# Rewritten units of a selective scan, with the gate behind the first scan of the next unit

## What is computed

```python
residual = hidden if residual is None else hidden + residual
hidden = rmsnorm(residual, norm_w[i])
# mamba_mixer: d = 64, dI = 128, 16 states, L = 256, batch 2
u, z = split(x @ in_w);  uc = silu(conv4(u) + cb)
dt_r, Bm, Cm = split(uc @ xp_w);  dt = softplus(dt_r @ dt_w + dt_b)
h = exp(dt * A) * h + (dt * u) * B_t;  y_t = einsum(h, C_t)     # over 256 steps
y = (y + u * Dp) * silu(z);  return y @ out_w
```

## Time and profile before

| | us |
|---|---|
| median of 3 runs | 383.29 |
| lowest, highest | 382.54, 387.21 |
| span of the profiled execution | 383.2 |
| VectorE busy | 291.4 (76%) |
| TensorE busy, weight loads | 321.3 (84%), 231.9 (61%) |
| ScalarE busy | 251.6 (66%) |
| GpSimd busy | 210.4 (55%) |

### The profile page before, as it was taken

How to read it: one execution, slowest core, us unless ns; L and a number is a source line. 1 busy time by engine, 2 the same in 40 slices (tenths; PEclk the granted TensorE clock), 3 DMA queues, 4 the chain that set the end, 5 groups by cost and what they waited for, 6 DMA issues and landing times.

```text
span 383.2 us, 5559 instructions
## 1 busy us (share of the span) xinstructions
PE 321.3 (84%) x1810; PEld 231.9 (61%) x1810; DVE 291.4 (76%) x508; ACT 251.6 (66%) x698; POOL 210.4 (55%) x182
## 2 busy tenths in 40 slices
PE   4866998899999998788979798797987979778674
PEld 3255775656557646566758576575856758556552
DVE  2675377868783525498988989899898998989453
...
GB/s 214 358 119 3 124 2 1 2 0 3 3 0 2 1 110 2 143 136 275 62 213 156 124 272 47 232 143 136 258 28 269 103 173 212 68 275 0 2 0 14
DMA packets 19750, 41.06 MB, mean 107 GB/s; under 512 B 7986, under 2 KB 10626, under 8 KB 19594
## 3 DMA queue, kind: packets, MB, share of 16 engines
...
HBM read 40.31 MB, written 0.39 MB: 106 GB/s over the span
## 4 chain that ended last, share of the span: by engine, by line
PE 37%; DVE 31%; POOL 11%; ACT 9%; issue 7%; DMA 2%; POOLq 1%; DVEq 0%; SPq 0%; ACTq 0%
DVE big L1148 14%; POOL big L1662 5%; PE PS L678 4%; PE PS L521 4%; DVE big L1139 4%; PE PS L291 2%; ACT PS L1460 2%; PE PS L297 2%; DVE big L1158 2%; PE PS L485 2%; POOL big L1563 2%; PE PS L415 2%; PE PS L585 2%; PE PS L495 2%; POOL rms L1638 2%
## 5 line engine op out<-in xcount | busy, mean ns | idle before, releaser
L1148 DVE TENSOR_TENSOR_SCAN big<-PS,big 128x1024 f32<-128x1024 f32 x48 | 108.4, 2281 | 1.0 <-DVE big L1139 0.2
L1460 ACT ACTIVATE PS<-unit_t,amat 128x255 f32<-128x255 f32 x192 | 81.6, 467 | 13.4 <-DVE unit_t L1123 9.0
L1671 POOL TENSOR_TENSOR big<-big 128x1024 f32<-128x1024 f32 x36 | 84.8, 2358 | 4.2 <-DVE big L1148 1.6
L678 PE MATMUL PS<-big,cst 128*128 128x256 f32 x288 | 66.5, 387 | 0.7 <-POOL big L1671 0.6
L678 PEld LDWEIGHTS PS<-big,cst 128*128 128x128 f32 x288 | 55.4, 194 | 9.9 <-POOL big L1671 2.2
L1662 POOL TENSOR_TENSOR big<-unit_t,big 128x1024 f32<-128x1024 f32 x24 | 57.4, 2396 | 5.7 <-issue 3.7
L1620 POOL TENSOR_TENSOR w2t<-w2t,w0t 128x768 f32<-128x768 f32 x2 | 3.6, 1807 | 92.3 <-DVE big L1078 92.3
L1264 ACT ACTIVATE big<-PS 128x512 f32<-128x512 f32 (+1 forms) x43 | 24.7, 583 | 25.2 <-PE PS L521 9.9
L646 PE MATMUL PS<-stack,pick_b 96*128 96x256 bf16 x144 | 22.2, 277 | 11.9 <-DVE big L1139 10.5
L1316 ACT ACTIVATE big<-PS,big 128x256 f32<-128x256 f32 x64 | 29.6, 473 | 1.5 <-DVE big L918 1.4
L1139 DVE TENSOR_TENSOR big<-unit_t,PS 128x1024 f32<-128x1024 f32 x24 | 29.0, 1208 | 0.5 <-PE PS L646 0.4
...
## 6 DMA issues: line engine op xcount, KB each, us to landing
...
```

Source lines behind the costliest of these rows:

```text
L678: pe.matmul(yps, ident, hc[:, g, s], start=False, stop=False)
L1148: v.tensor_tensor_scan(flat(hst[:, g]), flat(da[g % 2]), flat(dbu[:, g]), 0.0, ALU.mult, ALU.add).then_inc(sem("m_h"), 1)
L1460: one = act.activation(da[g % 2][:, n, 1:N], dt[u % 2][:, 1:N], ACT.Exp, scale=amat[:, u // 2, col:col + 1])
L1671: pool.tensor_tensor(hc[:, g], hst[:, g], csp[u % 2][:, SG * g:SG * (g + 1)], ALU.mult)\
```

## The change

VectorE: the gate of unit u - 1 moves from ahead of drive 0 to behind scan 0. softplus is approximated in another form: ScalarE does Abs, Tanh, Exp, Tanh instead of six operations, and VectorE one fused operation instead of two ahead of dt. dt now also waits until stack is complete.

TensorE: the transpose of hs is written as four plain f32 products (hs is no longer doubled to 128 columns; the second pair writes the shifted copy to partitions 64 to 127). The bf16 parts of xd are taken away in PSUM by `take_away`, between the sums. `spread_first` moves to the end of the unit before, `prep_in` behind `spread_last`, `sum_skip` ahead of the two idle products, and `sum_last` ahead of the second half of group 2's sum. `out_proj` of the unit before still stands ahead of `spread_second`.

ScalarE: hs is 64 columns wide, ht one operation for both halves of the partitions, each part of stack is one more copy of xd, and the decays stand in other places among them. GpSimd: `prep_split` goes, weigh 0 stands ahead of drive 3, and weigh 2 has two halves. The diff, without its constants, buffers, set-up on GpSimd and changed counts of semaphores:

```diff
@@ -618,7 +618,12 @@
-            last = pe.transpose(PS[:, 7, a * P:(a + 1) * P], hs2[b][:, a], ident)
+            one = hs2[b][:, a, 0:D]
+            pe.matmul(PS[0:D, 7, a * P:(a + 1) * P], one, ident, start=True, stop=True)
+            if a == 0:
+                last = pe.matmul(PS[D:P, 7, 0:P + 1], one, moved[:], start=True, stop=True)
+            else:
+                last = pe.matmul(PS[D:P, 7, P + 1:N], one, ident[:, 0:P - 1], start=True, stop=True)
@@ -637,6 +644,14 @@
+    def take_away(u, n):
+        pe.wait_ge(sem("m_xs"), 4 * u + 2 + n)
+        if n == 0:
+            pe.wait_ge(sem("m_sp"), 4 * u + 1)
+        pe.matmul(xd, less[:, n], stack[u % 2][:], start=False, stop=True, skip_group_check=True)\
+            .then_inc(sem("m_less"), 1)
@@ -663,27 +678,34 @@
-    def sum_skip(u, zs_of=None):
+    def sum_skip(u):
...
+        pe.wait_ge(sem("m_zs"), u + 1)
+        pe.matmul(yps, dmat[:, i], uc[b], start=True, stop=True)
+    def sum_y(u, g, zs_of=None):
+        pe.wait_ge(sem("m_hc"), 4 * u + g + 1)
...
-        pe.matmul(yps, dmat[:, i], uc[b], start=True, stop=False)
-    def sum_y(u, g):
-        pe.wait_ge(sem("m_hc"), 3 * u + g + 1)
...
-            pe.matmul(yps, ident, hc[:, g, s], start=False, stop=False)
+            pe.matmul(yps, ident, hc[:, g, s], start=False, stop=True, skip_group_check=True)
+    def sum_third(u, h):
+        pe.wait_ge(sem("m_hc"), 4 * u + 3 + h)
+        for s in range(2 * h, 2 * h + 2):
+            last = pe.matmul(yps, ident, hc[:, 2, s], start=False, stop=True, skip_group_check=True)
+        return last
     def sum_last(u):
...
-                last = pe.matmul(yps, ident, hc[:, NSG - 1, s], start=False, stop=(s == SG - 1))
-        last.then_inc(sem("m_y"), 1)
+                pe.matmul(yps, ident, hc[:, NSG - 1, s], start=False, stop=True, skip_group_check=True)
@@ -698,40 +720,56 @@
+    def idle_turns(count):
+        for _ in range(count):
+            pe.matmul(PS[:, 6, N:2 * N], zero_t[:, 0:1].to_broadcast([P, P]), CONST.of(cst, "rope")[:, 0:N],
+                      start=False, stop=True, skip_group_check=True)
     def keep_awake(count, bank=5):
...
     keep_awake(7, 6)
+    pe.wait_ge(sem("m_moved"), 4)
     prep_transpose(0)
     keep_awake(1)
     pe.wait_ge(sem("m_weights"), 5)
     prep_in(0)
     keep_awake(3)
     prep_x(0)
-    keep_awake(7)
+    take_away(0, 0)
+    keep_awake(1)
+    take_away(0, 1)
+    keep_awake(5)
+    spread_first(0)
     for u in range(UNITS):
         more = u + 1 < UNITS
         if u:
-            sum_y(u - 1, 2)
             sum_last(u - 1)
-        spread_first(u)
-        if u:
+            sum_third(u - 1, 1).then_inc(sem("m_y"), 1)
             out_proj(u - 1)
         spread_second(u)
+        sum_skip(u)
         if more:
-            keep_awake(2, 6)
+            idle_turns(2)
             prep_transpose(u + 1)
-            prep_in(u + 1)
         spread_last(u)
         if more:
+            prep_in(u + 1)
             prep_x(u + 1)
-        sum_skip(u, u + 1 if more else None)
-        sum_y(u, 0)
+        sum_y(u, 0, u + 1 if more else None)
+        if more:
+            take_away(u + 1, 0)
         sum_y(u, 1)
-    sum_y(UNITS - 1, 2)
+        if more:
+            take_away(u + 1, 1)
+        sum_third(u, 0)
+        if more:
+            spread_first(u + 1)
     sum_last(UNITS - 1)
+    sum_third(UNITS - 1, 1).then_inc(sem("m_y"), 1)
     out_proj(UNITS - 1)
     spare(1, 5)
@@ -1114,13 +1150,11 @@
     def prep_dt(u):
...
-        v.wait_ge(sem("m_sp"), 6 * u + 4)
-        v.scalar_tensor_tensor(sp_a, sp_3, LOG_D2, sp_u, ALU.add, ALU.mult).then_inc(sem("m_poly"), 1)
-        v.wait_ge(sem("m_sp"), 6 * u + 6)
-        v.wait_ge(sem("m_poly"), 2 * u + 1)
-        v.scalar_tensor_tensor(sp_v, sp_2, LOG_SCALE * LOG_D, sp_a, ALU.add, ALU.mult).then_inc(sem("m_poly"), 1)
-        v.wait_ge(sem("m_poly"), 2 * u + 2)
-        v.scalar_tensor_tensor(dt[b], dtp, 0.0, sp_v, ALU.max, ALU.add).then_inc(sem("m_dt"), 1)
+        v.wait_ge(sem("m_sp"), 4 * u + 4)
+        v.scalar_tensor_tensor(sp_l, sp_w, LOG_D / LOG_S, sp_u, ALU.add, ALU.mult).then_inc(sem("m_poly"), 1)
+        v.wait_ge(sem("m_poly"), u + 1)
+        v.wait_ge(sem("m_xs"), 4 * u + 4)
+        v.scalar_tensor_tensor(dt[b], dtp, 0.0, sp_l, ALU.max, ALU.add).then_inc(sem("m_dt"), 1)
@@ -1160,10 +1194,10 @@
     for u in range(UNITS):
         prep_dt(u)
+        drive(u, 0)
+        scan(u, 0)
         if u:
             gate(u - 1)
-        drive(u, 0)
-        scan(u, 0)
         drive(u, 1)
         scan(u, 1)
         if u + 1 < UNITS:
@@ -1394,19 +1428,14 @@
-            last = act.activation(hs2[b][:, a].rearrange("p (c e) -> p c e", c=2),
-                                  src.unsqueeze(1).to_broadcast([P, 2, D]), ACT.Copy,
-                                  scale=rms[b][:, a:a + 1])
+            last = act.activation(hs2[b][:, a, 0:D], src, ACT.Copy, scale=rms[b][:, a:a + 1])
...
     def prep_ht(u):
...
-        for c in range(2):
-            r = slice(64 * c, 64 * c + 64)
-            last = act.activation(ht[u % 2][r, 3 + c:3 + c + N], ups[r], ACT.Copy,
-                                  scale=cols[r, u // 2, DS + 3:DS + 4])
-        last.then_inc(sem("m_ht"), 1)
+        act.activation(ht[u % 2][:, 3:3 + N], ups, ACT.Copy, scale=cols[:, u // 2, DS + 3:DS + 4])\
+            .then_inc(sem("m_ht"), 1)
@@ -1432,22 +1461,20 @@
-    def prep_middle(u):
-        act.wait_ge(sem("m_rest"), u + 1)
-        act.activation(stack[u % 2][0:64], rest[:], ACT.Copy).then_inc(sem("m_xs"), 1)
+    def prep_part(u, n):
+        act.wait_ge(sem("m_less"), 2 * u + n)
+        act.activation(stack[u % 2][:], xd, ACT.Copy, scale=0.5).then_inc(sem("m_xs"), 1)
     def prep_softplus(u):
...
-        act.wait_ge(sem("m_sp"), 6 * u + 1)
-        act.activation(sp_u, sp_a, ACT.Exp, scale=-1.0).then_inc(sem("m_sp"), 1)
-        act.activation(sp_v, sp_a, ACT.Tanh, scale=0.5, bias=turn_t).then_inc(sem("m_sp"), 1)
-        act.wait_ge(sem("m_sp"), 6 * u + 3)
-        act.activation(sp_3, sp_u, ACT.Square, bias=a2_t).then_inc(sem("m_sp"), 1)
-        act.activation(sp_1, sp_v, ACT.Square, bias=a_t).then_inc(sem("m_sp"), 1)
-        act.wait_ge(sem("m_sp"), 6 * u + 5)
-        act.activation(sp_2, sp_1, ACT.Square, scale=LOG_ROOT, bias=b_t).then_inc(sem("m_sp"), 1)
+        act.wait_ge(sem("m_sp"), 4 * u + 1)
+        act.activation(sp_v, sp_a, ACT.Tanh, scale=LOG_K, bias=turn_t).then_inc(sem("m_sp"), 1)
+        act.activation(sp_u, sp_a, ACT.Exp, scale=-1.0, bias=logs_t).then_inc(sem("m_sp"), 1)
+        prep_part(u, 1)
+        act.wait_ge(sem("m_sp"), 4 * u + 2)
+        act.activation(sp_w, sp_v, ACT.Tanh, scale=LOG_M, bias=shift_t).then_inc(sem("m_sp"), 1)
@@ -1470,37 +1497,40 @@
     prep_softplus(0)
-    prep_middle(0)
     prep_z(0)
+    prep_part(0, 2)
     act.wait_ge(sem("m_weights"), 5)
     every = range(SG)
     for u in range(UNITS):
         more = u + 1 < UNITS
         decay(u, 0, every)
+        decay(u, 1, every[0:3])
         if u:
             act.wait_ge(sem("m_hid"), u)
         if u and more:
             prep_norm(u + 1)
         if u:
             keep_residual(u - 1)
-        decay(u, 1, every[0:2])
+        decay(u, 1, every[3:4])
         if u and more:
             prep_hs(u + 1)
-        decay(u, 1, every[2:4])
+        decay(u, 2, every[0:1])
         if more:
             prep_ht(u + 1)
-        decay(u, 2, every[0:3])
+        decay(u, 2, every[1:3])
         if more:
             prep_tu(u + 1)
         decay(u, 2, every[3:4])
         if more:
             prep_zs(u + 1)
-        decay(u, 3, every)
+        decay(u, 3, every[0:2])
         if more:
             prep_xd(u + 1)
+        decay(u, 3, every[2:4])
+        if more:
             prep_softplus(u + 1)
-            prep_middle(u + 1)
             prep_z(u + 1)
+            prep_part(u + 1, 2)
     act.preload_act_table_set("natural_log_exp_and_others")
     act.wait_ge(sem("m_hid"), UNITS)
     keep_residual(UNITS - 1)
@@ -1643,15 +1681,6 @@
-    def prep_split(u):
-        b = u % 2
-        pool.wait_ge(sem("m_xs"), 3 * u + 2)
-        pool.tensor_tensor(rest[:], xds[b][0:64], stack[b][0:64], ALU.subtract).then_inc(sem("m_rest"), 1)
-        pool.wait_ge(sem("m_xs"), 3 * u + 3)
-        pool.tensor_tensor(stack[b][32:64], rest[32:64], stack[b][32:64], ALU.subtract).then_inc(sem("m_stack"), 1)
-        pool.wait_ge(sem("m_stack"), u + 1)
@@ -1662,28 +1691,29 @@
-    def weigh(u, g):
+    def weigh(u, g, parts=1):
...
-        pool.tensor_tensor(hc[:, g], hst[:, g], csp[u % 2][:, SG * g:SG * (g + 1)], ALU.mult)\
-            .then_inc(sem("m_hc"), 1)
+        for n in range(parts):
+            s, size = SG // parts * n, SG // parts
+            pool.tensor_tensor(hc[:, g, s:s + size], hst[:, g, s:s + size],
+                               csp[u % 2][:, SG * g + s:SG * g + s + size], ALU.mult).then_inc(sem("m_hc"), 1)
...
-    prep_split(0)
...
     for u in range(UNITS):
```

(43 more changed lines are left out.)

## The result

The changed kernel took 401.06 us in the median of 4 runs (399.28 to 402.58) against 385.25 us for the kernel before (4 runs, 382.54 to 387.45); the ratio is 1.042, with a 95% interval of 1.036 to 1.049. It is slower, as forecast. The profiled execution had a span of 397.5 us (383.2 before). Some executions of a kernel showed a lower granted clock and took 1.5% longer or more; the medians count them, the ratios of this document leave them out.

A forecast was written before the change was run, and what follows sets the result against it. The prediction took VectorE's queue to bound the kernel before, with a gate-to-uc chain beside it. Its new period, 4.36 + 6.27 + 7.53 = 18.16 us against 16.32, gave 383.2 + 17.5 = 400.7 us, range 389 to 409.

The forecast's parts named there:

- What bounds the kernel before: VectorE's own queue sets the 16.32 us period; a second chain from gate to uc has 0.6 us to spare.
- the first rival: On VectorE, the removed work is simply gained: 1.63 us less a unit, 365 us in all; chance 5%.
- the third wait: On VectorE ahead of scan 3, for exponentials that ScalarE runs behind xds and stack: 0.6 us, on the path.
- From T to G: On VectorE, from the end of dt (T) to the end of the gate (G): 4.36 us.
- The wait behind the gate: On VectorE, drive 1 waits for the spread, which TensorE queues behind out_proj: 1.2 us of new wait.
- The chain to uc: From the gate's end through ScalarE, GpSimd and TensorE to the next unit's uc: 6.27 us.
- The term of the transposing products: On TensorE, between hs and ht: four plain products, eight passes, 1.11 us; bounds 0.44 and 1.56.
- From uc to T: On VectorE, from uc's start to the end of the next dt: 3.1 + 4.43 = 7.53 us.
- The wait at uc: On VectorE ahead of uc, for ScalarE's tanh: 1.6 us, the second new wait.
- The sum: Whole kernel: period 18.16 us against 16.32, +18.4 for units 1 to 10, -0.9 for unit 0; 400.7 us.
- A hidden chain: Gate to uc is hidden and the two other waits stay: 16.56 us a unit, 384.7 us; chance 8%.
- The clock rival: TensorE's clock falls while it waits for each gate: up to +2.3 us a unit, 424 us, or 412; chance 7%.

The follow-up runs named there:

- gate_front: The changed kernel with the gate where it was, ahead of drive 0; 396.16 us, ratio 1.023 to the kernel before.
- spread_ahead: The changed kernel with spread_second ahead of out_proj on TensorE; 397.30 us, ratio 1.024 to the kernel before.
- decay_whole: The changed kernel with the four exponentials of group 3 together, ahead of the copies xds and stack; 398.96 us, ratio 1.038 to the kernel before.
- mid_whole_gz: The changed kernel with the gate between drive 0 and scan 0, group 3's exponentials together, GpSimd's gz product behind the next unit's drive 2; 380.43 us, ratio 0.991.
- gate_mid: The changed kernel with the gate between drive 0 and scan 0; 383.99 us, ratio 1.005 to the kernel before.
- gate_only: The kernel before with only the gate moved behind scan 0, nothing rewritten; 461.64 us, ratio 1.194 to the kernel before.

## Why the prediction was right

It said 400.7 us and a period of 18.16 us; the median was 401.06 us and the period 17.75. Step by step:

- *What bounds the kernel before*: this reading was wrong, though no term of the sum hangs on it, only the price of the first rival. "VectorE's own queue sets the period" does not fit a queue that waits 0.82 us in every unit: the gate waits for the sum over states, so the loop closes through other engines. In gate_front, with less work on VectorE, that wait grew to 2.02 us, and the period with it; the 1.63 us "gained" were not seen.
- *What the loss is put down to*: the sum holds for the two changes together and does not tell them apart. With the gate at its old place the rewritten units already cost 1.04 us, by gate_front's reading through the third wait and a later sum. Behind scan 0 the later sum is covered, and the chain behind the later gate costs in its place.
- *From T to G*: 4.36 forecast, 4.43 measured (267.48 - 263.05).
- *The wait behind the gate*: 1.2, measured 1.19; that it lies inside the loop and is covered by the chain, spread_ahead showed.
- *The chain to uc*: 6.27, measured 5.75. The term of the transposing products was mis-sized: 1.11 and 0.04 of handing over, measured 0.71 from their start to ht's (270.39 to 271.10). I took eight passes one behind the other; they ran four and four beside each other. The measured time lies inside the stated bounds of 0.44 and 1.56. That the two halves overlap was not among the reasons given for the lower bound. tanh came 1.18 behind prep_in's start instead of 1.26. The rest stood within 0.06 us.
- *From uc to T*: 3.10 + 4.43 forecast, 3.17 + 4.40 measured. decay_whole showed that the third wait is on the path and that removing it alone brings a new cost. The wait at uc was 1.01 us for 1.6 foreseen, by the shorter chain.
- *The sum*: the forecast period was 0.41 us too long, 4.1 us over ten units. Two things made up for part of it: two units with a fallen clock (+1.7), and the first and last periods. The first period was 15.63, not 14.9: five products that keep the clock stand ahead of spread_first(0), and drive 0 waited 0.59 us for it, which I had costed at 0. The last stretch took 0.7 more. Against that, the first dt came 2.25 us earlier, which was costed at 0; the last section shows that this start varies from run to run. In the traces the difference is 14.3 us, not 17.5; the medians differ by 15.8, and that of the kernel before had risen to 385.25 us from the 383.2 that the forecast starts from. So the median lies 0.4 us from the forecast by luck; the difference was forecast 1.7 us too high.
- *The rivals*: that the removed work is simply gained was refuted, by gate_front and most plainly by mid_whole_gz. A hidden chain did not occur at this place of the gate; at gate_mid's place it nearly did. The clock rival was true in small: 1.8 us of waiting foreseen, 1.71 measured, and two falls that cost 0.83 us each, not 2.3 a unit; in gate_only it was the largest single term (23.87 us for 19.71). One of the prediction's own signs of being wrong, a granted clock that leaves 1.00, thus came true in two units.

The first unit in the changed kernel's trace, VectorE (answers to the first and second T of the earlier trace rows):

```profile
157.42 0.42 DVE L1157 SCALAR_TENSOR_TENSOR unit_t<-PS,big 128x256 f32<-128x256 f32 x1 [0.67 <-ACT stack L1467]
...
158.89 1.22 DVE L1173 TENSOR_TENSOR big<-unit_t,PS 128x1024 f32<-128x1024 f32 x1 [0.59 <-PE PS L661]
...
168.94 2.29 DVE L1182 TENSOR_TENSOR_SCAN big<-PS,big 128x1024 f32<-128x1024 f32 x1 [0.56 <-ACT PS L1487]
...
173.05 0.42 DVE L1157 SCALAR_TENSOR_TENSOR unit_t<-PS,big 128x256 f32<-128x256 f32 x1
```
